# Routing weights of two expert stages spread by DMA from DRAM instead of by a selection product

## The reference, cut to what matters

```
scores = softmax(x @ gw + gb)                 # 32 experts
cw[t, e] = the score where e is one of the 4 chosen experts, else 0
y = sum over e of cw[t, e] * ((silu(x @ w1[e] + b1[e]) * (x @ w3[e] + b3[e])) @ w2[e] + b2[e])
z = (silu(x @ sw1 + sb1) * (x @ sw3 + sb3)) @ sw2 + sb2     # shared expert, weight 1
```

## Time and profile before

| | us |
|---|---|
| median of 3 runs | 1516.19 |
| lowest and highest of them | 1511.08, 1522.08 |
| the profiled execution, its own time | 1522.68 |
| its span, first to last instruction | 1520.9 |

### The profile page before, as it was taken

One profiled execution on the slowest core, in us unless ns is written; L12 is line 12 of the kernel. 1 busy time (PEld: TensorE's weight loads), 2 busy tenths in 40 slices (PEclk: granted clock), 3 DMA queues, 4 the chain that ended last, 5 costly groups with the idle time before them and its releaser, 6 DMA issues. The chain is left out here.

```text
span 1520.9 us, 23123 instructions
## 1 busy us (share of the span) xinstructions
PE 1294.4 (85%) x8332; PEld 754.7 (50%) x8332; DVE 716.3 (47%) x998; ACT 767.6 (50%) x1136; POOL 550.0 (36%) x725
## 2 busy tenths in 40 slices
PE   3599999995899948158999999999999838898997
PEld 3233333333677737024455555555555426686776
DVE  5420000003455565126746666666666315565756
ACT  0455555544444421025747777777776635343443
POOL 1333333334554430101323343333422338454544
PEclk8665555557999975557959999999999969999999
DMA  3200000004000003557757887878865042000000
GB/s 139 116 26 25 26 25 25 14 5 147 1 0 0 0 6 134 201 185 226 218 143 209 227 214 224 241 216 224 226 215 176 7 143 86 0 0 0 0 0 28
DMA packets 119933, 155.76 MB, mean 102 GB/s; under 512 B 27806, under 2 KB 110880, under 8 KB 119840
## 3 DMA queue, kind: packets, MB, share of 16 engines
q1 hardware_dynamic: 101280, 145.30, 30.2%
q0 software_dynamic: 18560, 9.23, 4.0%
HBM read 81.97 MB, written 72.34 MB: 101 GB/s over the span
## 5 line engine op out<-in xcount | busy, mean ns | idle before, releaser
L1010 DVE TENSOR_REDUCE a_part<-a_duo 128x2 f32<-128x1024 f32 x256 | 311.4, 1225 | 202.2 <-PE a_duo L874 201.4
L972 ACT ACTIVATE a_probs<-a_duo 128x1024 f32<-128x1024 f32 x256 | 261.7, 1022 | 106.6 <-PE a_duo L913 101.0
L1252 POOL TENSOR_TENSOR f_hid_lo<-f_hid,f_hid_hi 128x512 fp32r<-128x512 f32 (+1 forms) x168 | 216.2, 1289 | 203.0 <-ACT f_hid_hi L1233 203.0
L819 POOL DMA_DIRECT2D scr_y1c<-a_y x256 | 131.4, 521 | 326.5 <-DVE a_y L1001 325.3
L623 ACT ACTIVATE a_probs<-a_duo 128x1024 f32<-128x1024 f32 x192 | 154.0, 811 | 137.3 <-PE a_duo L581 137.1
L968 ACT ACTIVATE a_rel<-a_rel_ps 128x384 f32<-128x384 f32 x256 | 125.9, 492 | 140.2 <-PE a_rel_ps L856 119.9
L601 PE MATMUL a_acc<-a_probs,a_v 128*32 128x256 f32 (+1 forms) x1280 | 182.8, 569 | 2.7 <-issue 2.7
L928 PE MATMUL a_acc_ps<-a_probs,a_v 128*32 128x256 f32 x2048 | 169.2, 403 | 0.3 <-issue 0.2
L856 PE MATMUL a_rel_ps<-a_emb_all,a_q 24*128 24x384 f32 x256 | 122.4, 478 | 53.8 <-DMA a_kb<-scr_kb 31.0
L570 POOL TENSOR_TENSOR a_probs<-a_probs,const 128x256 f32<-128x256 f32 x128 | 94.6, 742 | 193.8 <-ACT a_probs L623 193.4
L581 PE MATMUL a_duo<-a_q,a_k 24*128 24x512 f32 (+3 forms) x384 | 125.8, 656 | 17.9 <-DMA a_k<-scr_k 16.6
(11 more groups left out here) (199 smaller groups left out, 2139.3 us busy)
## 6 DMA issues: line engine op xcount, KB each, us to landing
scr_rel<-a_rel SPq DMA_DIRECT2D x128, 384.0 KB, 3.7
a_rel_raw<-scr_rel SPq DMA_DIRECT2D x128, 384.0 KB, 4.2
f_raw<-in_w SPq DMA_DIRECT2D x33, 192.0 KB, 2.7
scr_q<-q_hi SPq DMA_DIRECT2D x4, 1024.0 KB, 7.8
scr_y1c<-a_y POOLq DMA_DIRECT2D x256, 8.0 KB, 3.3
a_q<-scr_q SPq DMA_DIRECT2D x40, 96.0 KB
a_k<-scr_k SPq DMA_DIRECT2D x32, 96.0 KB
a_q<-scr_q POOLq DMA_DIRECT2D x24, 96.0 KB, 4.8
```

The lines of the kernel that those rows point to most:

```text
L819: pool.dma_start(scr["y1c"][w, b, head, :, at:at + QUARTER], ys[32 * (2 * hd + c) + HD * w:32 * (2 * hd + c) + HD * (w + 1), h % 2, :]).th ...
L972: act.activation(probs[:, n % 4, :], bank_pair("t", n)[:], ACT.Exp, scale=SCALE).then_inc(exp_done, 1)
L1010: dve.tensor_reduce(part[:, h % 2, x, :, j % 4], bank_pair("s", m)[:].rearrange("p (h t) -> p h t", h=2), AX.X, ALU.max, negate=True).then ...
L1252: pool.tensor_tensor(hid_lo[0:m, c % 4, :], hid[0:m, c % 2, :], f32(hid_hi[0:m, c % 4, :]), ALU.subtract).then_inc(lo_ready, 1)
```

## The change

The routing weights stay in plain fp32. ScalarE copies them from PSUM to a tile `cwT`, one DMA writes that tile to DRAM (`scr["cw"]`) at the end of the attention stage, and SyncE waits for it. In the expert stage SyncE reads, for each token tile and chunk, the row of each expert that owns rows of the chunk, repeated over these rows (a step of 0 in DRAM), into one of four buffers `share`. VectorE takes `share` in place of the PSUM result `c`. The product with `sel`, the loading and rounding of `sel`, the fp32r split of the weights and the split of `b2` go; the bias of layer 0 is one plain fp32 product.

```diff
-def weights_hi(router, sb, act, banks):
+def weights_saved(router, sb, act, banks):
     E = router.layer.E
     for c in range(NC):
         act.wait_ge(router.cw_turned, c + 1)
-        if c == 0:
-            act.wait_ge(router.cw_done, 1)
-        act.activation(sb["cw_split"][0:E + 1, c * CH:(c + 1) * CH], banks[c][0:E + 1, :], ACT.Copy).then_inc(router.cw_hi_done, 1)
-
-
-def weights_lo(router, sb, dve, banks):
+        act.activation(sb["cwT"][0:E + 1, c * CH:(c + 1) * CH], banks[c][0:E + 1, :], ACT.Copy).then_inc(router.cw_saved, 1)
+
+
+def weights_stored(router, sb, scr, sp):
     E = router.layer.E
-    for c in range(NC):
-        cols = slice(c * CH, (c + 1) * CH)
-        dve.wait_ge(router.cw_hi_done, c + 1)
-        dve.tensor_tensor(sb["cw_split"][LO_ROW:LO_ROW + E + 1, cols], banks[c][0:E + 1, :],
-                          f32(sb["cw_split"][0:E + 1, cols]), ALU.subtract).then_inc(router.cw_done, 1)
+    sp.wait_ge(router.cw_saved, NC)
+    sp.dma_start(scr["cw"][0:E + 1, :], sb["cwT"][0:E + 1, :]).then_inc(router.cw_stored, 16)
+    sp.wait_ge(router.cw_stored, 16)
...
-            pool.memset(f32(sb["cw_split"][:]), 0.0).then_inc(router.cw_done, 1)
...
                 for hd in range(2):
                     store(2 * pair + 1, hd)
+            weights_stored(router, sb, scr, sp)
             for s in range(2):
                 sp.wait_ge(y_stored[s], 64 * PAIRS)
...
-        raw = tile("raw", [P, 2, 4, GRP * P])
+        raw = tile("raw", [P, 2, 3, GRP * P])
...
-        sel = tile("sel", [P, wide], F32R)
+        WB = 4
+        share = tile("share", [P, WB, CH])
...
-                sp.dma_start(b2[LO_ROW:LO_ROW + E + 1, :], d["b2"]).then_inc(small, 16)
...
+            def share_out(ti, c):
+                last = ti * K + c - WB if c >= WB else (ti - 1) * K + uses(c % WB)[-1]
+                if last >= 0:
+                    sp.wait_ge(hid_ready, last + 2)
+                for e, a, b in owners(c):
+                    row = scr["cw"][e:e + 1, ti * CH:(ti + 1) * CH]
+                    sp.dma_start(share[a:b, c % WB, :], bass.AP(row.tensor, row.offset, [[0, b - a], [1, CH]])).then_inc(share_loaded[c % WB], 16)
+
             load(0)
             load(1)
+            for c in range(WB):
+                share_out(0, c)
...
-            for n in range(2, len(groups)):
-                load(n)
+            pending = list(range(2, len(groups)))
+            for ti in range(NC):
+                for c in range(K):
+                    if pending and c in starts[:-3]:
+                        load(pending.pop(0))
+                    if ti or c >= WB:
+                        share_out(ti, c)
...
                     pe.matmul(u, w_lo[1][:, ch], sb["x_hi"][:, cols], start=False, stop=False)
-                    pe.matmul(u, w_hi[1][:, ch], sb["x_lo"][:, cols], start=False, stop=True)
-                    pe.matmul(w, sel[:, ch], sb["cw_split"][:, cols], start=True, stop=True).then_inc(u_ready, 1)
+                    pe.matmul(u, w_hi[1][:, ch], sb["x_lo"][:, cols], start=False, stop=True).then_inc(u_ready, 1)
...
-                    pe.matmul(y_ps[:], b2_hi[:], sb["cw_split"][:, cols], start=True, stop=False)
-                    pe.matmul(y_ps[:], b2_lo[:], sb["cw_split"][:, cols], start=False, stop=False)
+                    pe.matmul(y_ps[:], b2[0:E + 1, :], sb["cwT"][0:E + 1, cols], start=True, stop=False)
...
-                    u, w, g = u_ps[c % 2][0:m, :], c_ps[c % 2][0:m, :], gate[0:m, c % 2, :]
+                    u, w, g = u_ps[c % 2][0:m, :], share[0:m, c % WB, :], gate[0:m, c % 2, :]
...
                     dve.wait_ge(up_ready, n + 1)
+                    dve.wait_ge(share_loaded[c % WB], (ti * shares_each(c) + shares_before(c)) * 16)
                     if c >= 2:
                         dve.wait_ge(lo_ready, ti * K + c - 1)
                     dve.tensor_tensor(hid[0:m, c % 2, :], w, up[0:m, c % 2, :], ALU.mult).then_inc(hid_ready, 1)
```

More of the change, by code:

```diff
@@ L1052, in experts @@
         w_lo = [tile(f"w{m}_lo", [P, wide], F32R) for m in (1, 3, 2)]
-        sel = tile("sel", [P, wide], F32R)
+        WB = 4
+        share = tile("share", [P, WB, CH])
         if k == 0:
             b1, b3 = tile("b1", [P, K]), tile("b3", [P, K])
-            b2 = tile("b2", [P, D]); b2_hi = tile("b2_hi", [P, D], F32R); b2_lo = tile("b2_lo", [P, D], F32R)
+            b2 = tile("b2", [P, D])
         gate = tile("gate", [P, 2, CH]); up = tile("up", [P, 2, CH]); hid = tile("hid", [P, 2, CH])
@@ L1069, in pb @@
             return ctx.enter_context(nc.psum_tensor(f"f{k}_{name}", [P, CH], F32))
-        g_ps, u_ps, c_ps = [pb(f"g{i}") for i in range(2)], [pb(f"u{i}") for i in range(2)], [pb(f"c{i}") for i in range(2)]
+        g_ps, u_ps = [pb(f"g{i}") for i in range(2)], [pb(f"u{i}") for i in range(2)]
         y_ps, z_ps = pb("y"), pb("z")
@@ L1075, in experts @@
         small, att_loaded, att_ready, step = sem("small"), sem("att_loaded"), sem("att_ready"), sem("step")
-        bias_ready, quotient_step = sem("bias_ready"), sem("quotient_step")
+        quotient_step = sem("quotient_step")
+        share_loaded = [sem(f"share_loaded{s}") for s in range(WB)]
         g_ready, u_ready, gate_ready, up_ready, hid_ready = sem("g_ready"), sem("u_ready"), sem("gate_ready"), sem("up_ready"), sem("hid_ready")
@@ L1079, in experts, with owners, uses, shares_before @@
         y_ready, turned, out_ready, out_stored = sem("y_ready"), sem("turned"), sem("out_ready"), sem("out_stored")
-        names = [("w1", 0), ("w3", 1), ("w2", 2), ("sel", 3)]
+        names = [("w1", 0), ("w3", 1), ("w2", 2)]
+        inter = (R - CK[-1]) // E if k == 0 else 176
+        def owners(c):
+            r, out = c * P, []
+            while r < c * P + CK[c]:
+                e = min(r // inter, E)
+                end = min((e + 1) * inter if e < E else R, c * P + CK[c])
+                out.append((e, r - c * P, end - c * P))
+                r = end
+            return out
+        def uses(s):
+            return [c for c in range(K) if c % WB == s]
+        def shares_before(c):
+            return sum(len(owners(i)) for i in uses(c % WB) if i <= c)
+        def shares_each(c):
+            return sum(len(owners(i)) for i in uses(c % WB))
         block = ctx.enter_context(nc.Block())
@@ L1130, in raw_count @@
         def raw_count(n):
-            return sum(len(pieces(m, *groups[g])) for g in range(n % 2, n + 1, 2) for m in range(4))
+            return sum(len(pieces(m, *groups[g])) for g in range(n % 2, n + 1, 2) for m in range(3))
         def split_hi(eng, n, copy):
@@ L1136, in split_hi @@
             eng.wait_ge(raw_loaded[n % 2], 16 * raw_count(n))
-            for m in range(4):
+            for m in range(3):
                 for rows, a, b in pieces(m, c0, c1):
-                    ins = copy((*w_hi, sel)[m][0:rows, a:b], raw[0:rows, n % 2, m, a - c0 * P:b - c0 * P])
+                    ins = copy(w_hi[m][0:rows, a:b], raw[0:rows, n % 2, m, a - c0 * P:b - c0 * P])
             ins.then_inc(raw_hi, 1)
@@ L1272, in _ @@
             if k == 0:
[L1273 to L1278, removed]
                 dve.wait_ge(att_loaded, 16)
@@ L1336, in two_layers @@
             "v": tile("v", [P, N]),
-            "cw_split": tile("cw_split", [P, N], F32R),
+            "cwT": tile("cwT", [P, N]),
             "yT": tile("yT", [P, N]),
```

20 lines of the change are left out of this document (10 added, 10 removed).

## The result

| | before | after | ratio |
|---|---|---|---|
| first comparison, medians of 4 and 4 runs, us | 1514.72 | 1591.19 | 1.0526 [1.0479, 1.0572] |
| again on another chip, 23 and 4 runs, us | 1511.91 | 1588.54 | 1.0486 [1.0414, 1.0559] |
| span of the profiled execution, us | 1520.9 | 1598.5 | |

What follows compares the result with a forecast made beforehand. The prediction took TensorE's ten products a chunk as the bound, with GpSimd's `hid_lo` close behind; 21 + 6 - 3 + 1.7 - 2 = +24 us on the median 1516.2 gave 1540 us, range 1504 to 1564.

Steps and rivals of the forecast that it cites:

- The steady chunks: Chunks outside the first tile's loads, a tile's first three and the division: 2.50 us each, +21 us in all.
- The cycle: In a steady chunk `hid`, `hid_hi`, `hid_lo` and the next, blocked `hid` follow one another: 2.59 us together.
- The store of layer 0: End of layer 0's attention stage: SyncE resumes later because it waits for the weights' store, +1.7 us (0.5 to 6).
- the two orders: In steady chunks either `hid_lo` goes first, 2.59 us a chunk, or `hid` does, 2.20 us; 2.50 taken.
- rival 2: Steady chunks: `hid` wins the port at every second chunk, pitch 2.20 us, kernel 1506 us; chance 0.14.
- rival 3: Something starves: share reads come one at a time, +200 us, or TensorE's clock drops, +270 us; chance 0.05.
- First tiles: Each layer's first tile: `hid` and the L1147 instructions contend for the port, +0.7 us a three-chunk group, +6 us (-4 to +15).
- Tile starts: Eight tile starts: chunks filling the pipe lose one product, 0.43 us, and no `hid_lo` is left to block: -3 us.
- Layer 1's store: End of layer 1's attention stage: the 17-row store, estimated at 6.4 us, lies under 13.4 us of cover: zero.
- Start of layer 1: Start of layer 1's expert stage: one transfer of sel less ahead of the first rounding, and its 0.29 us: -1 us.
- VectorE's added wait: Between `up` and `hid`: the reads have long landed when VectorE waits for them, so it costs zero.
- the bias: Layer 0's tile starts: a plain fp32 product takes 0.91 us against 0.82; zero, at most +4 us in all.

Runs made afterwards that it cites:

- a_wait_early: The changed kernel with VectorE's wait for the arrived share put ahead of `up` instead of between `up` and `hid`: 1570.87 us, ratio 1.0395.
- a_again: The changed kernel timed once more, unchanged, on another chip: 1588.54 us, ratio 1.0486 to the kernel before.
- a_up_psum: The changed kernel with `up` in two PSUM banks, so that `hid` reads SBUF once: 1519.84 us, ratio 1.0013.
- a_ends: The changed kernel with the store split into 16 rows and one, layer 1's two 1 MB loads issued later, layer 0's bias product issued earlier: 1567.45 us, ratio 1.0362.
- a_no_reads: The changed kernel with share rows read for the first four chunks only and VectorE's wait against a constant: 1574.29 us, ratio 1.0366.

## Why the prediction was wrong

**What held.** The steady chunks, which carried the sum: forecast 2.50 us a chunk, measured 2.51 and 2.53, so 43 x 0.20 + 57 x 0.26 = +23 against +21. The cycle came as built: 0.03, 0.63, 0.08, 1.28, 0.56, pitch 2.58. The Trainium skill's rule (SBUF — State Buffer, Who interferes with whom) that the first holds the port for its whole instruction would give 2.72; the 0.55 us by which `hid` ends after `hid_lo` speak for the row again. The store of layer 0 came to +1.8 (forecast +1.7), and VectorE never waited for `share`. Some of it is luck. 2.50 was a guess at how the two orders mix, and the order was shifted by a wait that the forecast put at zero: with it moved away (`a_wait_early`) the pitches are 2.49 and 2.43 us, 43 x 0.18 + 57 x 0.16 = +17. The order of rival 2 came too, at one chunk in four of layer 0 and one in eight of layer 1. Of rival 3 the clock stayed at 1.00 in the steady chunks only.

**First tiles, +6.** This failed. They took +18 (16 without their ten steady chunks). Two steps were wrong. I charged the price of the meeting to `hid`, half of it behind idle time. It fell on the weights' splits: with `hid` coming in between, L1179 took 3.84 us instead of 2.96, 0.9 us in nearly every group, some 9 us in both layers. And I took the earlier trace rows, a clock of 1.00 at 85%, for the whole stage. The longer split and the two products fewer ahead of `fall` let TensorE stand for 1.36 + 0.88 + 0.46 = 2.70 us, and the products behind that ran at the lower level; so `gate`, `hid_hi` behind it and GpSimd's `hid_lo` came 1.04 us later, which is the whole growth of its wait from 1.73 to 2.77 us. In layer 1 it happened behind four waits of 2.34 to 2.70 us, in layer 0 once, some 6 us in all; in the group whose wait was 1.92 us the clock stayed at 1.00 and GpSimd waited 1.74 us. It isn't the same in each execution: `a_again` has three such stretches in layer 1, and a wait of 2.78 us without one. `a_up_psum` takes all of it back.

**Tile starts, -3, "no `hid_lo` is left to block".** This failed, with +16 in six tiles. Two mistakes. The bias row says x2: two instructions, so by my own rate 2 x 0.91 = 1.82 us stood against 0.82, and not 0.91; measured 2.00. The that I took the rate from are transpositions, each one instruction; the product takes two. I had the right value only as the upper end: 1.18 us in three tiles, 3.5 us, more than before. And the last two chunks of a tile have nothing beside them, so a late `hid_lo` is paid in full; TensorE waits 1.62 and 1.61 us where it waited 1.03 and 1.04, and its last products of the tile already run at the lower level (0.43 us apart), where in the same tile before they ran at the higher. In layer 1 the last chunk after and before:

```profile
1443.50 0.63 PE L1211 MATMUL f_y<-f_hid_hi,f_w_hi 96*128 96x512 f32 x1 [1.61 <-POOL f_hid_lo L1282]
1443.93 0.63 PE L1212 MATMUL f_y<-f_hid_hi,f_w_lo 96*128 96x512 f32 x1
```

```profile
1381.89 0.47 PE L1180 MATMUL f_y<-f_hid_hi,f_w_hi 96*128 96x512 f32 x1 [1.04 <-POOL f_hid_lo L1252]
1382.20 0.39 PE L1181 MATMUL f_y<-f_hid_hi,f_w_lo 96*128 96x512 f32 x1
```

**Layer 1's store, "13.4 us of cover, worth zero".** This failed, +4.0. The Trainium skill's rule (DMA: Bandwidth & Descriptors, Why a DMA increments its semaphore by 16 and not by 1) gives one DMA engine for 17 rows. The trace agrees: the packets went one after another, in 5.8 us where I estimated 6.4. Most of the cover wasn't there. Of the 13.4 us only the first 3.6 were SyncE's wait for the attention's own stores (L787), beside which the new store could run; the other 9.8 (L660, 9.7 after) start when SyncE's waits end, and move with them. The reading of the earlier trace rows was the error.

**Start of layer 1, -1.** This failed, +5.0. I followed the loads behind waits, and not those ahead of them: group 2's weights already stood behind the two 1 MB loads, and now stand behind six share reads as well, whose issue alone takes 2.81 us. `a_ends` gives back 5.0 by moving the two loads away, with the share reads in place; that the six reads cost the 5.0 is the likely reading, and no run takes them alone away.

**VectorE's added wait, 0.** This failed, though the steady chunks hide it. The data have long landed, and still 0.20 us go by between `up` and `hid` where it was 0.03. With it `hid_lo` stretches `hid` at seven of eight chunks of layer 1; early, the wait gives back 0.1 us a chunk, and layer 1's tiles 2 to 4 are 6.8 us shorter.

Of the 52 us by which the forecast fell short, by the profiled executions some 25 are contention in first tiles and tile ends, with the lower clock level that it brought, 4 the bias, 10 the store and start of layer 1 and 2 the steady chunks. So the steps that failed are those outside the steady chunk: first tiles, tile ends, the bias, the store and the start of layer 1. Some 10 stay open; scatter of preparation and attention between executions is as large.

## What to carry to other kernels

When an operand moves from PSUM to SBUF, ask who else reads SBUF at that moment; the price was 72 us here, more than four times what the removed product was worth, and one moved buffer took it back. Price the filling and the ends of a pipeline apart from its steady step: a link that is longer by 0.56 us costs more there than in the middle, and a longer wait of TensorE there can cost its clock level besides. Before a wait is called covered, see whether the work that covers it starts before the wait or after it.

## What the runs showed that I had not expected

- A semaphore wait on a value computed from the loop counter, long satisfied, put 0.20 us between two VectorE instructions that stood 0.03 us apart. It was 0.03 again with the wait on a constant (`a_no_reads`) and with the wait ahead of the first (`a_wait_early`). Two other waits on computed values stand at the same place in every kernel here, so why this one costs is open.
- A small shift in time changes the contended order: with 0.20 us more, `hid_lo` stretches `hid` at seven of eight chunks of layer 1 (2.53 us on average); without them `hid` is first at every third (2.98, 2.10, 2.20).
- In the first tile of layer 1 TensorE's mean granted clock was 0.85 (0.90 in `a_again`), where it was 0.93 before and 0.95 with `up` in PSUM: part of the price of contention between two other engines came through its clock.
- The share reads keep the DMA engines 35% busy at 105 GB/s beside the steady chunks of layer 1, and the pitch of layer 1 shows nothing of it: 2.44 us without them, 2.43 with them and the early wait.
